# A fused transformer kernel on one core: key projection of the first batch ahead of the layer norm's transposes in three 16-head attention stages

## The reference, cut to what matters

```python
x = x + jnp.tanh(g_xattn[0]) * _L0_xattn_ref(_layernorm(x), ctx_1024, ctx_1024, Wq, bq, Wk, bk, Wv, bv, Wo, bo)   # a0
x = x + jnp.tanh(g_xattn[1]) * _L1_xattn_ref(ctx_1024, ctx_1024, _layernorm(x), mask, W_v, W_o)                   # a1
x = x + jnp.tanh(g_xattn[3]) * _L3_xattn_ref(_layernorm(x), ctx_1024, ctx_1024, valid_lens, Wq, Wk, Wv, Wo)       # a3
# inside: q = proj(queries), k = proj(ctx), v = proj(ctx), 16 heads of 8;
# softmax(q k / scale, masked) v, heads joined, times Wo
```

## Time and profile before

| | us |
|---|---|
| median of 3 runs | 5829.42 (5827.53 to 5834.3) |
| the profiled execution | 5833.64 |
| its span | 5831.9 |
| start of stage a0, a1, a3 (first DMA issue) | 14.53, 1678.04, 4351.62 |
| first score maxima of a0, a1, a3 | 56.54, 1723.64, 4392.34 |
| KB issued by SP at the start of a0, a1, a3 | 1841, 3002, 2582 |

### The profile page before, as it was taken

How to read it: one execution, slowest core, us unless ns; L and a number is a source line. 1 busy time by engine, 2 the same in 40 slices (tenths; PEclk the granted TensorE clock), 3 DMA queues, 4 the chain that set the end, 5 groups by cost and what they waited for, 6 DMA issues and landing times. The chain is left out here.

```text
span 5831.9 us, 109941 instructions
## 1 busy us (share of the span) xinstructions
PE 5276.3 (90%) x39878; PEld 3466.6 (59%) x39878; DVE 3851.6 (66%) x10948; ACT 3100.1 (53%) x4492; POOL 1589.2 (27%) x1360
## 2 busy tenths in 40 slices
PE   6999999997959999999999988979458999999996
PEld 4666666665835555555555547857355666666663
DVE  5666666665766766766766657756466676767674
ACT  3666666664624444444444445634145666666664
POOL 3222222221442222222222214500352222222220
PEclk9999999998979999999999998989578999999998
DMA  3323333332233323333332315479223232323230
GB/s 86 77 67 77 70 75 78 71 72 60 58 87 91 82 72 78 82 76 74 82 79 71 82 40 108 77 198 252 82 91 77 68 76 67 77 67 78 67 72 13
DMA packets 160603, 475.40 MB, mean 82 GB/s; under 512 B 34721, under 2 KB 85724, under 8 KB 159867
## 3 DMA queue, kind: packets, MB, share of 16 engines
q1 hardware_dynamic: 148738, 449.69, 32.5%
q0 software_dynamic: 11328, 18.72, 1.1%
HBM read 237.66 MB, written 19.88 MB: 44 GB/s over the span
## 5 line engine op out<-in xcount | busy, mean ns | idle before, releaser
L692 DVE CUSTOM_DVE_ANT_0 a_dump<-a_max,a_mqf 100x482 f32<-100x482 f32 (+1 forms) x1536 | 978.5, 657 | 426.5 <-PE a_max L883 395.6
L1635 PE MATMUL a_max<-a_stack,a_qblk 96*128 96x482 f32 (+1 forms) x2304 | 1030.4, 449 | 28.7 <-DMA a_stack<-a_khi 17.6
L1473 DVE CUSTOM_DVE_ANT_0 a_dump<-a_max,a_penq 128x482 f32<-128x482 f32 (+3 forms) x1248 | 783.0, 655 | 409.1 <-PE a_max L1635 386.9
L1466 DVE TENSOR_REDUCE a_mx<-a_max 128x1 f32<-128x482 f32 (+3 forms) x1248 | 779.6, 654 | 406.6 <-PE a_max L1635 283.4
L565 ACT ACTIVATE a_probs<-a_scores 128x800 f32<-128x800 f32 (+1 forms) x768 | 643.2, 838 | 657.4 <-PE a_scores L900 657.2
L1368 ACT ACTIVATE a_probs<-a_scores,a_kbias 128x800 f32<-128x800 f32 (+1 forms) x768 | 697.3, 926 | 404.1 <-PE a_scores L1662 404.1
L1662 PE MATMUL a_scores<-a_qblk,a_stack 128*128 128x400 f32 (+1 forms) x3072 | 832.9, 353 | 40.6 <-POOL a_qblk L1283 34.0
L1370 ACT ACTIVATE a_probs<-a_scores 128x800 f32<-128x800 f32 (+1 forms) x768 | 624.7, 836 | 410.0 <-PE a_scores L1662 406.0
L883 PE MATMUL a_max<-a_stack,a_qblk 96*100 96x482 f32 (+1 forms) x1536 | 712.1, 485 | 39.5 <-DVE a_mx L692 27.6
L1674 PE MATMUL a_pv<-a_probs,a_v_aug 128*32 128x200 f32 x12288 | 705.7, 341 | 3.0 <-ACT a_probs L1368 2.1
L1662 PEld LDWEIGHTS a_scores<-a_qblk,a_stack 128*128 128x128 f32 (+1 forms) x3072 | 548.3, 184 | 185.0 <-POOL a_qblk L1283 57.6
(11 more groups left out here) (554 smaller groups left out, 8473.0 us busy)
## 6 DMA issues: line engine op xcount, KB each, us to landing
a_stack<-a_khi SPq DMA_DIRECT2D x768, 180.5 KB, 3.3
a_ctxT<-in_ctxT_dram SPq DMA_DIRECT2D x128, 722.0 KB, 14.3
a_stack<-a_klo SPq DMA_DIRECT2D x384, 180.5 KB, 3.5
f_wb<-weights_by_token SPq DMA_DIRECT2D x16, 1600.0 KB
a_ctxn<-in_ctxn_dram SPq DMA_DIRECT2D x32, 704.0 KB
a_mt_i<-in_mask1T_dram SPq DMA_DIRECT2D x32, 600.0 KB, 6.9
a_mq_i<-in_mask_dram SPq DMA_DIRECT2D x32, 564.1 KB
a_mask_i<-in_mask_dram SPq DMA_DIRECT2D x32, 541.5 KB
```

The costliest lines, as they stand in the source:

```text
L692: nc.vector.tensor_tensor_reduce(dump[:, k % 2, 0:n], src, mqf[:, b % 2, o:o + n], 1.0, -3.0e38, ALU.mult, ALU.max, out_).then_inc(mx_free, 1)
L1466: nc.vector.tensor_reduce(out_, src, AX.X, ALU.max).then_inc(mx_free, 1)
L1473: nc.vector.tensor_tensor_reduce(dump[0:rows, k % 2, 0:n], src, penq[0:rows, b % 2, o:o + n], 1.0, -3.0e38, ALU.add, ALU.max, out_).then_i ...
L1635: pe.matmul(to[:, 0:n], qblk[0:96, b % 2, at:at + D], stack[0:96, b % 2, g, o:o + n], start=True, stop=True).then_inc(mx_full, 1)
```

## The change

In the three stages the projection of batch 0's keys on PE and its copies on ACT stand ahead of the layer norm's square root, transposes and copies. wk, wv and the key bias are loaded first and have their own semaphore `kv_in`; the other weights keep `weights_in`. The padding memset of `ctxT` has its own semaphore `pad_ready`, waited for ahead of the value projection; POOL raises `consts_ready` by 4 instead of 3 in one go. The lists of POOL and DVE are otherwise untouched. Shown for `attention_phase`; `packed_attention_phase` is changed alike (its own line numbers, no mask):

```diff
-        loads = [(wq[:, :, :], w["wq"]), (wk[:, :], w["wk"]), (wv[:, :], w["wv"]), (wo[:, :], w["wo"]),
-                 (blk[:, :], w["blk"])]
+        kv_loads = [(wk[:, :], w["wk"]), (wv[:, :], w["wv"])]
+        loads = [(wq[:, :, :], w["wq"]), (wo[:, :], w["wo"]), (blk[:, :], w["blk"])]
...
-            loads += [(bq[:, :], w["bq"]), (bk[:, :], w["bk"]), (bv[:, :], w["bv"]), (bo[:, :], w["bo"])]
+            kv_loads += [(bk[:, :], w["bk"])]
+            loads += [(bq[:, :], w["bq"]), (bv[:, :], w["bv"]), (bo[:, :], w["bo"])]
...
-        weights_in = sem("weights_in")
+        kv_in, weights_in, pad_ready = sem("kv_in"), sem("weights_in"), sem("pad_ready")
...
-        LOADED = 16 * len(loads)
+        KV_LOADED, LOADED = 16 * len(kv_loads), 16 * len(loads)
...
             ctx_load(0)
+            for dst, src in kv_loads:
+                sp.dma_start(dst, src).then_inc(kv_in, 16)
             for dst, src in loads:
                 sp.dma_start(dst, src).then_inc(weights_in, 16)
             ctx_load(1)
...
-            pool.memset(ctxT[:, :, KEYS:KT * D], 0.0).then_inc(consts_ready, 1)
+            pool.memset(ctxT[:, :, KEYS:KT * D], 0.0).then_inc(pad_ready, 1)
...
-            pool.sem_inc(consts_ready, 3)
+            pool.sem_inc(consts_ready, 4)
...
         @block.scalar
         def _(act):
-            act.wait_ge(var_ready, 1)
-            act.activation(tmp[:, 3, :], tmp[:, 0, :], ACT.Sqrt).then_inc(root_ready, 1)
-            for n in range(NBLK):
-                act.wait_ge(turned, n + 1)
-                act.activation(xnT[:, n * TOK:(n + 1) * TOK], p_turn[n % 2][:, 0:TOK], ACT.Copy).then_inc(stored, 1)
-            act.wait_ge(weights_in, LOADED)
...
+            act.wait_ge(kv_in, KV_LOADED)
             k_evac("k0", 0)
             k_evac("k12", 0)
+            act.wait_ge(var_ready, 1)
+            act.activation(tmp[:, 3, :], tmp[:, 0, :], ACT.Sqrt).then_inc(root_ready, 1)
+            for n in range(NBLK):
+                act.wait_ge(turned, n + 1)
+                act.activation(xnT[:, n * TOK:(n + 1) * TOK], p_turn[n % 2][:, 0:TOK], ACT.Copy).then_inc(stored, 1)
+            act.wait_ge(weights_in, LOADED)
             act.wait_ge(consts_ready, CONSTS)
             q_round(0)
...
         @block.tensor
         def _(pe):
-            for n in range(NBLK):
-                if n >= 2:
-                    pe.wait_ge(stored, n - 1)
-                for j in range(BLK):
-                    pe.wait_ge(xn_ready, n * BLK + j + 1)
-                    ins = pe.transpose(p_turn[n % 2][:, j * S:(j + 1) * S], xn[:, n % 2, j, :], ident[0:S, 0:S])
-                ins.then_inc(turned, 1)
-            pe.wait_ge(weights_in, LOADED)
...
+            pe.wait_ge(kv_in, KV_LOADED)
             k_proj("k0", 0)
             k_proj("k12", 0)
+            for n in range(NBLK):
+                if n >= 2:
+                    pe.wait_ge(stored, n - 1)
+                for j in range(BLK):
+                    pe.wait_ge(xn_ready, n * BLK + j + 1)
+                    ins = pe.transpose(p_turn[n % 2][:, j * S:(j + 1) * S], xn[:, n % 2, j, :], ident[0:S, 0:S])
+                ins.then_inc(turned, 1)
+            pe.wait_ge(weights_in, LOADED)
             pe.wait_ge(consts_ready, CONSTS)
             pe.wait_ge(stored, NBLK)
             q_proj(0)
+            pe.wait_ge(pad_ready, 1)
             v_proj("v01", 0)
```

More of the change, by code:

```diff
@@ L1310, in _ @@
         def _(act):
[L1311 to L1316, removed]
             def k_evac(job, b):
@@ L1574, in _ @@
         def _(pe):
[L1575 to L1582, removed]
             def ring(*job):
```

## The result

| | before | after |
|---|---|---|
| median, us | 5829.42 (5827.53 to 5834.3, 7 runs) | 5809.02 (5806.17 to 5814.44, 7 runs) |
| profiled execution (span) | 5833.64 (5831.9) | 5809.02 (5807.2) |
| start of a0, a1, a3 | 14.53, 1678.04, 4351.62 | 14.16, 1664.51, 4331.48 |
| start to first maxima, a0, a1, a3 | 42.0, 45.6, 40.7 | 33.3, 41.8, 37.8 |
| length of a0, a1, a3 | 1360.6, 1797.1, 1421.5 | 1350.4, 1792.9, 1417.0 |

The ratio is 0.9965, 95% interval 0.9953 to 0.9977: faster by 20.4 us, with an interval of 13.4 to 27.4. The forecast was 5814.2 and the case was the forecast's; the time came out 5.2 us better, which lies inside that interval. A stage's length here runs from its first statistics instruction (BATCH_NORM) to that of the next stage; that of a3 runs to the first load of the last block, and so includes 25.2 us of a layer norm that the change leaves alone.

What follows compares the result with a forecast made beforehand. Stage starts in a0, a1, a3 hang on one chain to the first score maxima, no engine being full. Gains 11.2, 5.7 and 5.2 (22.1) less 6.9 of slip save 15.2 us: 5829.42 becomes 5814.2, range 5804 to 5823.

Steps and rivals of the forecast that it cites:

- Key branch: Start of a0, a1, a3: key inputs land at start + 4.7, copies end at + 11.8, before the variance is ready.
- rival C: Stage starts: ACT and TensorE stand until the first context lands, only with all start transfers; slower, 5832 us; chance 0.04.
- Rival B: Stage starts: key inputs land later, say start + 8, or value products stay slow; 8 to 11 saved, 5820; chance 0.15.
- Stack loads hidden, queries next: Ahead of first maxima: stack loads leave the path, queries become late; gains 11.2 in a0, 5.7 in a1, 5.2 in a3.
- The query branch: In a0, from the start of the query projection to the first maxima: 6.2 us.
- The surcharge: Query projection: eight products run at the slow clock, as the key projection no longer warms TensorE directly ahead; 0.9 us.
- The slip: Layer norm on DVE: POOL's low parts hold L121 and all behind it, 2.3 us per stage, 6.9 in three.
- rival A: Layer norm: no slip, or the mask product finds the fast clock; 22 to 25 saved, 5806 us; chance 0.15.
- The table load: Load for the square root on ScalarE moves behind the copies; costed at nothing, between 0 and 1.3 per stage.
- The sum: Three stages together: 22.1 us gained less 6.9 lost to POOL holding the layer norm, 15.2 saved.
- After the first maxima all runs relative to them: Rest of each stage: batch 1's keys, loads and queries hang on the maxima's loop, so the shift is kept.
- Rival D: Loops behind the stage starts were waiting for something else, so the gain is given back; 5829 us; chance 0.06.

Runs made afterwards that it cites:

- Experiment 4: Changed kernel, but ScalarE and TensorE wait ahead of the key projection for all weights and the second context too; ratio 0.999 to the kernel before.
- experiment 1: Changed kernel, but POOL's first low parts wait for all 32 normalising steps; ratio 0.9971 to the kernel before.
- experiment 3: Changed kernel with ScalarE's square root ahead of the key copies again; ratio 0.9969 to the kernel before.
- experiment 7: Changed kernel with the edits of experiment 3, experiment 5 and experiment 6 together; ratio 0.9939 to the kernel before.
- experiment 5: Changed kernel with the TENSOR_SCALARs ahead of the square root rewritten as two-input steps or folded away; ratio 0.9971 to the kernel before.
- experiment 8: Changed kernel and that of experiment 7, unaltered, side by side on one chip: 5813.17 and 5796.62 us, kernel before 5833.12.
- experiment 2: Kernel before plus nine key products that nobody reads, after batch 0's value products, to keep TensorE busy; ratio 1.0 to the kernel before.
- experiment 6: Changed kernel with POOL's two memsets of the stack's ones-rows moved to before and after batch 1's low parts; ratio 0.9959 to the kernel before.
- experiment 2, second version: Kernel before plus key products that nobody reads, thirteen in a0, nine in a1 and a3; ratio 0.9995 to the kernel before.

## Why the prediction was right

**Key branch**: right. Landing at start + 5.05 (predicted 4.7), copies done at +11.3 (11.8), low parts at 28.06 (28.3). Experiment 4 shows that the early landing was the condition for about half of the gain or more, as rival C had it. Rival B fell with the landing: +5 us, not +8.

**Stack loads hidden, queries next**: right. No stack DMA ends a wait ahead of the first maxima any more. The query branch from the last copy to the maxima, 41.35 to 47.46, took 6.1 (6.2). The surcharge was right in kind and a little too large: the eight projections took 1.62 us instead of 0.98, 0.64 more where I had 0.9, since I took the price of a slow product from one with 144 columns and these have 100. The value products took 4.37 instead of 2.87, and they ended at 47.28, only 0.18 us ahead of the maxima, so they were close to becoming the end.

**The slip**: right in kind, a little too small. I took L121 as the step that stands and 2.3 us. It was L119, a step with two SBUF inputs, and the norm steps started 2.67 later (start + 17.87 instead of + 15.20; 2.6 in a1 and a3). That is what the Trainium skill says (SBUF — State Buffer, Who interferes with whom: a VectorE step with two SBUF inputs is blocked by a GpSimd instruction that reads SBUF); the three rows of L119 with 2.86, 2.80 and 2.80 us agree with it, and its 2.7 was the better term. Experiments 1, 3 and 7 tie it to POOL, and rival A, no slip, fell.

**The table load**: right at nothing, and simpler than I weighed. The Trainium skill (ScalarE: Activation LUTs, What ACT_TABLE_LOAD costs) adds a drain to the load, some 2.66 us in all. Where nothing else held the root, it followed 1.29 us after the load's start (25.72 to 27.01 in experiment 5, 30.23 to 31.52 in experiment 4), so no drain shows in these rows.

**The sum**: 15.2 predicted from start to maxima, 15.4 measured (8.7 + 3.8 + 2.9, predicted 8.9 + 3.4 + 2.9). That they meet so closely is partly luck: the slips came to 7.9 us and not 6.9, and in a1 the mask product took 5.02 us instead of the 5.65 assumed. In the second profile of the same kernel it took 6.04 (experiment 8); the length of that product hangs on where in it the clock rises (3.37 in experiment 2 with the clock up, 5.65 before).

**After the first maxima all runs relative to them**: this step was wrong: the three stages gained 3.5 us behind their first maxima, which I had at nothing. It left the clock out, which accounts for 2.4 of them: before, the maxima ran at 0.50 because of the very idling that the change removes. I had charged the change for the clock that the query projections lose and had not credited it for the clock that the maxima win, 1.6 us in a0 and 0.8 in a3 by the stretch up to the first score product. The other 1.1, and what the untouched stages gave, are not settled; they are of the size by which single profiles differ. Nor does this step explain the whole 5.2 us between forecast and median. With intervals of 13.4 to 27.4 us saved in the first result and 10.5 to 24.5 in experiment 8, the 15.2 that I had forecast and the 20 that were measured can't be told apart. Rival D, the gain given back, fell: the stages' lengths shrank by at least as much as the time to their first maxima.

## What to carry to other kernels

When a branch is moved forward, ask what else runs on the queue or port that it now meets: here POOL's low parts landed on the layer norm, and some 2.6 us in each of three stages, 7.9 in all, were lost beside the 15.4 gained. Where several obstacles stand in a row, test them together too: three edits that brought the first maxima forward by -1.0, 1.7 and 4.4 us alone (sum of the three stages) brought them forward by 16.4 together. And an idle TensorE ahead of a loop can cost twice, once in waiting and once in the slow clock behind it: here 1.3 to 2.5 us in a0 and up to some 3.4 in a3.

## Of the hardware, not expected

- GpSimd writing only holds VectorE's one-input TENSOR_SCALAR on 32 elements until the memset that is running has ended (L111 2.05 us, L116 3.98, against 0.18 in experiment 6; at 4.91 us each the two memsets of the kernel after end at 22.78 and 27.74, L111 at 22.82 and L116 at 27.78), but not a step with two SBUF inputs (0.19 us in experiment 5). GpSimd reading SBUF holds both kinds (L119 2.86, L120 3.25), and a CAST (2.94).
- The hold goes both ways, by and large in the order in which the two begin. A step of VectorE that began behind the low parts, or up to 0.05 us ahead of them, stood until they ended, even as one of 32 that follow each other with no pause, and the low parts kept 3.22 to 3.30 us (experiments 3 and 7). Behind a TENSOR_SCALAR on 1444 elements that had begun 0.12 us earlier the low parts took 3.93 us (experiment 2, second version). The kernel before has it too: in a3 the next GpSimd step, L1254, took 1.51 us beside L1451, against 1.02 to 1.06 in all its other executions.
